# Loads of the down weights issued by ScalarE in place of SyncE, in a kernel of attention and a Hadamard FFN

## The reference

```python
x = x + LN(attention(LN(x)))     # 16 heads of 32, low-rank queries and values, rotary, softmax
x = x + LN(ffn(LN(x)))

def ffn(x):                      # 512 -> 2048 -> 512
    x = fwht(x * SU_ug) / 64
    up, gate = x @ W_up.T * (Wscale_ug[:2048] * 64), x @ W_gate.T * (Wscale_ug[2048:] * 64)
    x = fwht(silu(gate) * up * SU_dp) / 64
    return x @ W_down.T * (Wscale_dp * 64)
```

## Time and profile before

| | before |
|---|---|
| median of 3 runs | 2013.04 us (2004.34, 2013.72, 2013.04) |
| the profiled execution's own time | 2004.77 us |
| its span, first to last instruction | 2002.9 us |
| TensorE's granted clock over the span | 0.987 of 2.4 GHz |
| busy: PE, DVE, ACT, POOL | 94%, 64%, 55%, 47% |
| DMA engines, mean over the span | 140 GB/s |

### The profile page before, as it was taken

The page is one execution under the profiler, slowest core; times in us unless marked ns, Lnnn a source line. Parts: engine busy times, 40 slices in busy tenths (PEclk is TensorE's granted clock), DMA queues, the critical chain, the costliest instruction groups (busy, mean ns, idle before and its releaser), DMA issues.

```text
span 2002.9 us, 59647 instructions
## 1 busy us (share of the span) xinstructions
PE 1884.5 (94%) x24393; PEld 1364.1 (68%) x24393; DVE 1275.5 (64%) x2141; ACT 1094.4 (55%) x1731; POOL 937.6 (47%) x958
## 2 busy tenths in 40 slices
PE   2688999999999999999999999999999999999997
PEld 0355555777777777777767777777677776777786
DVE  6788666766677667666667667666666666654322
ACT  3557998555565554555556555555555555554221
POOL 3625545454465445544555446534555445443422
PEclk9799999999999999999999999999999999999999
DMA  8655623664457445664566445744556446533644
GB/s 222 193 153 129 168 51 72 163 145 121 121 147 177 116 119 139 155 162 121 137 171 150 127 112 140 176 121 136 138 149 161 121 130 157 138 107 107 192 140 128
DMA packets 353029, 280.95 MB, mean 140 GB/s; under 512 B 285216, under 2 KB 286496, under 8 KB 351776
## 3 DMA queue, kind: packets, MB, share of 16 engines
q1 hardware_dynamic: 343536, 265.83, 51.6%
q10 hardware_dynamic: 9264, 11.61, 2.0%
HBM read 189.30 MB, written 20.98 MB: 105 GB/s over the span
## 4 chain that ended last, share of the span: by engine, by line
PE 76%; DVE 6%; DMA 6%; SPq 5%; ACT 3%; issue 3%; ACTq 1%; POOL 1%; POOLq 0%; DVEq 0%
PE ps L842 29%; PE ps L866 14%; PE ps L784 5%; PE ps L772 5%; PE ps L796 5%; PE ps L812 4%; DMA qT<-tok 4%; PE ps L831 4%; SPq L592 3%; PE ps L686 2%; PE ps L817 2%; PE ps L738 2%; DVE mx L1326 1%; PE ps L674 1%; PE ps L750 1%
## 5 line engine op out<-in xcount | busy, mean ns | idle before, releaser
L1016 ACT ACTIVATE pr<-ps,exp_scale 128x1024 f16<-128x1024 f32 x256 | 285.4, 1115 | 360.3 <-PE ps L796 341.7
L1326 DVE TENSOR_REDUCE mx<-ps 128x2 f32<-128x1024 f32 x256 | 312.4, 1224 | 213.1 <-PE ps L784 211.9
L1437 POOL TENSOR_TENSOR pr<-p,pr 128x512 f16<-128x512 f32 x256 | 297.5, 1162 | 316.1 <-ACT p L1022 316.0
L842 PEld LDWEIGHTS ps<-x2T,gate_w 128*128 128x128 f16 x6144 | 362.3, 98 | 46.1 <-issue 10.7
L842 PEld LDWEIGHTS ps<-x2T,up_w 128*128 128x128 f16 x6144 | 359.6, 98 | 42.0 <-issue 13.4
L842 PE MATMUL ps<-x2T,gate_w 128*128 128x128 f16 x6144 | 387.3, 220 | 0.2 <-DVE room L1373 0.2
L842 PE MATMUL ps<-x2T,up_w 128*128 128x128 f16 x6144 | 386.9, 219 | 0.3 <-issue 0.2
L866 PE MATMUL ps<-room 128*128 128x512 f16 x1536 | 376.9, 382 | 6.6 <-POOL room L1465 5.4
L1465 POOL TENSOR_TENSOR room<-room 128x256 f16<-128x256 f32 x256 | 172.9, 675 | 309.9 <-ACT room L1052 308.9
L1047 ACT ACTIVATE room<-ps,half_gate 128x256 f32<-128x256 f32 x256 | 121.8, 476 | 265.9 <-PE ps L842 265.3
L1340 DVE TENSOR_TENSOR pr<-ps,pr 128x512 f16<-128x512 f32 x256 | 175.2, 685 | 115.1 <-ACT ps L1027 115.1
(11 more groups left out here) (191 smaller groups left out, 2446.2 us busy)
## 6 DMA issues: line engine op xcount, KB each, us to landing
room<-down_mid SPq DMA_DIRECT2D x256, 512.0 KB, 3.6
xr<-in_x SPq DMA_DIRECT2D x34, 256.0 KB, 4.0
y_mid<-xr SPq DMA_DIRECT2D x32, 256.0 KB, 2.3
room<-y_mid ACTq DMA_DIRECT2D x32, 256.0 KB, 2.8
xa<-in_x SPq DMA_DIRECT2D x30, 256.0 KB, 3.5
out<-room SPq DMA_DIRECT2D x24, 256.0 KB, 2.9
x2T<-in_W_gate SPq DMA_DIRECT2D x5, 1024.0 KB, 5.6
gate_w<-in_W_down SPq DMA_DIRECT2D x4, 1024.0 KB, 6.9
```

The lines of the kernel that those rows point to most:

```text
L842: mm = nc.tensor.matmul(ffn_ps[i % 2][:, col:col + P], weights[:, chunks[j // 4], kt, pw, j % 4 * P:(j % 4 + 1) * P], x2T[:, px, kt, t * P ...
L1016: nc.scalar.activation(pr[:, U % 2, 0].rearrange("p (j h) q -> p j (h q)", j=2), work[k], ACT.Exp, scale=exp_scale[:, 0:1]).then_inc(p_hi. ...
L1326: nc.vector.tensor_reduce(mx[:, 2 * tp:2 * tp + 2, h], work[k], AX.X, ALU.max).then_inc(sm_freed.sem, 1)
L1437: nc.gpsimd.tensor_tensor(lo, p32[:], hi, ALU.subtract).then_inc(p_low.sem, 1)
```

## The change

SP's lists lose every `wl` and SP's block loses the function. ScalarE's block gets it, without the wait for `down_done`, and `hid_` calls it at its end, so the load of item i is issued right behind ScalarE's step `hid.i`. The same function is also added to GpSimd's block, where nothing calls it. All other steps keep their places.

```diff
@@ ORDER, SP
-        wl.3@-1 stk.2.1 wl.4@-1 xl.0@1 wl.5@-1 xl.1@1 wl.6@-1 wl.7@-1 ln1.0@1 xl.2@1 wl.8@-1 wl.9@-1 ln1.1@1 xl.3@1
-        stq.2 wl.10@-1 rl.0 stk.3.0 wl.11@-1 ln1.2@1 stk.3.1 wl.12@-1 ln1.3@1 wl.13@-1 wl.14@-1 wl.15@-1 wl.16@-1
...
+        stk.2.1 xl.0@1 xl.1@1 ln1.0@1 xl.2@1 ln1.1@1 xl.3@1
+        stq.2 rl.0 stk.3.0 ln1.2@1 stk.3.1 ln1.3@1
...
@@ FRONT, SP
-        stk.0.1@1 raw.10 stq.0@1 raw.11 stk.1.0@1 stk.1.1@1 oe.0 rl.2 oe.1 oe.2 ln2.0 rl.3 wl.0 ln2.1 oe.3 wl.1 ln2.2
-        stq.1@1 wl.2 stk.2.0@1 ln2.3
+        stk.0.1@1 raw.10 stq.0@1 raw.11 stk.1.0@1 stk.1.1@1 oe.0 rl.2 oe.1 oe.2 ln2.0 rl.3 ln2.1 oe.3 ln2.2
+        stq.1@1 stk.2.0@1 ln2.3
@@ block.sync
-            def wl(b, i):
-                if first(b) and i < 2:
-                    sp.wait_ge(q_filled, 48)
-                    for k in range(2):
-                        sp.wait_ge(put[k], 16 * 8)
-                else:
-                    sp.wait_ge(*down_done.at(b, i - 2))
-                sp.dma_start(wr[:, i % 2], down_dram[i % (NJ // 2)].rearrange("p (j w n) -> p j w n", j=2, w=2)).then_inc(
-                    w_in[i % 2].sem, 16)
@@ block.scalar
+            def wl(b, i):
+                if first(b) and i < 2:
+                    sc.wait_ge(q_filled, 48)
+                    for k in range(2):
+                        sc.wait_ge(put[k], 16 * 8)
+                sc.dma_start(wr[:, i % 2], down_dram[i % (NJ // 2)].rearrange("p (j w n) -> p j w n", j=2, w=2)).then_inc(
+                    w_in[i % 2].sem, 16)
+
             def hid_(b, i):
                 sc.wait_ge(*f_freed.at(b, i))
                 sc.wait_ge(*down_done.at(b, i - 2))
                 nc.scalar.activation(hid[:, i % 2, 0, :], act[:, i % 2, :], ACT.Copy).then_inc(h_hi.sem, 1)
+                wl(b, i)
```

More of the change, by code:

```diff
@@ L119 @@
     SP="""
-        wl.3@-1 stk.2.1 wl.4@-1 xl.0@1 wl.5@-1 xl.1@1 wl.6@-1 wl.7@-1 ln1.0@1 xl.2@1 wl.8@-1 wl.9@-1 ln1.1@1 xl.3@1
-        stq.2 wl.10@-1 rl.0 stk.3.0 wl.11@-1 ln1.2@1 stk.3.1 wl.12@-1 ln1.3@1 wl.13@-1 wl.14@-1 wl.15@-1 wl.16@-1
-        wl.17@-1 stq.3 wl.18@-1 stk.0.0@1 wl.19@-1 stk.0.1@1 wl.20@-1 wl.21@-1 wl.22@-1 wl.23@-1 wl.24@-1 wl.25@-1
-        stq.0@1 wl.26@-1 rl.1 wl.27@-1 stk.1.0@1 wl.28@-1 stk.1.1@1 oe.0 fe.1@-1 wl.29@-1 oe.1 rl.2 wl.30@-1 ln2.0
-        wl.31@-1 rl.3 wl.0 ln2.1 wl.1 ln2.2 oe.2 oe.3 fe.2@-1 stq.1@1 wl.2 stk.2.0@1 fe.3@-1 ln2.3
+        stk.2.1 xl.0@1 xl.1@1 ln1.0@1 xl.2@1 ln1.1@1 xl.3@1
+        stq.2 rl.0 stk.3.0 ln1.2@1 stk.3.1 ln1.3@1
+        stq.3 stk.0.0@1 stk.0.1@1
+        stq.0@1 rl.1 stk.1.0@1 stk.1.1@1 oe.0 fe.1@-1 oe.1 rl.2 ln2.0
+        rl.3 ln2.1 ln2.2 oe.2 oe.3 fe.2@-1 stq.1@1 stk.2.0@1 fe.3@-1 ln2.3
     """,
@@ L613, in fe @@
                 sp.dma_start(out_v[b, t], yt[:, t % 2, :]).then_inc(out_done[t % 2].sem, 16)
-            parts = dict(lda=lda, ldv=ldv, wput=wput, wget=wget, ldx=ldx, raw=raw_, dst=dst, wl=wl, xl=xl, rl=rl, ln1=ln1, ln2=ln2, stk=stk, stq=stq, oe=oe, fe=fe)
+            parts = dict(lda=lda, ldv=ldv, wput=wput, wget=wget, ldx=ldx, raw=raw_, dst=dst, xl=xl, rl=rl, ln1=ln1, ln2=ln2, stk=stk, stq=stq, oe=oe, fe=fe)
             ahead = next(i for i, (b, s) in enumerate(FRONT["SP"]) if s[0] not in ("lda", "xl"))
```

## The result

The changed kernel takes 2179.14 us (median of 4 runs, 2162.27 to 2184.16) against 2009.62 for the kernel before on the same chip: **8.3% slower**, ratio 1.0825, interval [1.0779, 1.0871]. Forecast was 2060 us, with a range of 2024 to 2095. The sign was right; the loss of 170 us is three and a half times the 47 forecast.

The account below looks back on a forecast made before the run. TensorE was taken to bound the kernel. Terms of 33 - 21 + 11 + 20 + 5 = +48 us on the profiled execution gave 2060 us against the 2013 us median, range 2024 to 2095.

Parts of the forecast that it names:

- What bounds the kernel: Whole kernel: TensorE, busy for 94% of the span; only what makes it wait, or frees it, moves the time.
- ScalarE's issue, zero: ScalarE's 256 load issues of 0.344 us mostly hide behind `hid` computing; upper bound 88 us, taken as zero.
- Quiet price: From the start of `hid.i` to the first matmul with no transposition in flight: 3.4 us, ends 3.2 and 3.7.
- The sum for the tail: Batch 7, where FFN items run alone: late weights at short distances cost +20 us (14 to 27).
- Shortages in the loop, 5.5 us a pass: Six loop passes: late weights stall TensorE 5.5 us a pass, +33 us in all (15 to 60).
- What SP gives back: Loop passes: the queries' transposition is issued earlier without SP's loads, 3.5 us a pass, -21 us; bounds 0 and 26.
- Batch 6, +11: Unrolled back, 1690 to 1865 us: shorter distances, so late weights cost +11 us.
- Clock, +5: Longer TensorE waits in batches 6 and 7 bring half clock, three times 1.7: +5 us (0 to 10).
- rival C: Descriptor generator locked, so loads issued beside SP's transposition issues hold ScalarE: 36 us more, 2096 us; chance 0.05.
- E: Loads beside transpositions land at 6.7 us, SP's gain is nil: 2109 at the far end, 2085 to 2100 likelier; chance 0.15.
- Its sign of being wrong: Landings of 5 us and more with transpositions later than today would show the forecast wrong through crowding.
- B's relief: SP's relief at the queries' waits in the passes outweighs lateness: all 26 us back, 2001 us; chance 0.07.

Follow-up runs that it names:

- plain copies: Transpositions replaced by plain copies of as many bytes, softmax scale zero: 1985.97 us for the kernel before, 2042.32 us for the changed kernel.
- ScalarE at the old moments: Against the kernel before, ScalarE issues the loads, but at the moments at which SP did: 2001.3 us, ratio 0.9967.
- The guards: The changed kernel, with SP issuing three transpositions of each pass only when a load of ScalarE has landed: 2128.58 us, ratio 1.0615.
- the smaller pieces: The changed kernel with each partition's 4096 B of a load in pieces of 2048 B or 1024 B: 2135.89 us and 2130.92 us.
- the swap: The changed kernel with ScalarE's step reordered: wait for down.(i-2), issue the load, then wait for gate-up and make high halves: 2104.06 us.

## Why the prediction was wrong

By its own steps:

- **What bounds the kernel**: right. TensorE's waits, with the half clock behind them, took all of the loss; the busy time of VectorE, ScalarE and GpSimd stayed within 6 us.
- **ScalarE's issue, zero**: right in size (0.331 us at the median). But it hides more than I said: ScalarE's sequencer sends the load 0.29 us (median) before `hid` computes, up to 1.7 us where `hid` waits its turn, since the issue needs nothing of `hid`. I had "it can't start before `hid.i`". At items 5 and 6, for which stalls of 0.3 and 0.8 were summed, it is 0.93 us ahead, and they have none.
- **Quiet price, 3.4 us from `hid` to the matmul**: right. In batch 7, where TensorE waited for weights, it was 3.35 us at the median. The sum for the tail came out by two errors that cancel: its gaps are 20.1 us, of which 5.0 were there before, so 15 added and not 20; the half clock behind them makes it 24 on the stretch, where 5 were given to the clock in the whole kernel. That this total is right is luck in part.
- **Shortages in the loop, 5.5 us a pass**: the term for lateness was about right (4.3 with plain copies), though split otherwise: item 9 has 2.3, not 1.2. What failed is the upper bound for a load beside a transposition, "ends 3.7 and 6.7". Those landings come from a kernel in which the loads of the down weights leave early and stand in one queue with the transpositions; the changed kernel alters both. Item 11 was given a stall of 1.5 and has 6.2; items 10, 3 and 4, not in the sum, land in up to 14 us. The loop's gaps ahead of `down` are 83 us, not 33: **this is the step that failed**.
- **What SP gives back, -21**: wrong in sign. With ScalarE at the old moments SP did give something back, 1.8 us a pass in the loop instead of 3.5. In the changed kernel the wait at group 2 rises from 2.47 to between 3.7 and 8.8 us. The prediction said that the bytes "still move in the same stretch" but still priced the gain from SP's issues alone: the loads gone from ahead of the transposition came back beside it (item 3's is issued 0.65 us behind it and lands in 11.4 us in the pass from 1094.3, the transposition in 12.7).
- **Batch 6, +11**: 17, of which 13.7 are added gaps; the same mechanism in small.
- **Clock, +5**: 50 us of busy time is the real figure. It follows the waits, as in the earlier trace rows, but all along the loop, where I had taken the half clock as going away.
- **The lock rule (rival C)**: false here. ScalarE's load at 1163.62 was issued in 0.33 us inside SP's transposition issue of 6.42 us from 1161.59, as rows 8 had it. The Trainium skill (Perfetto Trace Analysis, DMA Instruction, HWDGE) has the generator locked for one sequencer at a time; the runs show no such hold. Of the 256 loads 49 were issued inside a transposition's issue, in 0.331 us at the median, as outside; three of them took 1.1 to 1.8 us, and those too were over before the transposition's issue was.
- **The rivals**: E (crowding, 0.15) named the mechanism, loads beside transpositions slow and transpositions delayed, but took 6.7 us as its worst landing and 2109 us as its far end. The slow landings turned out at 8 to 18 us. Its sign of being wrong, landings of 5 us and more with later transpositions, is what came. B's relief is what the run with early loads shows, at 0.3%.

In sum: +170 us is roughly +56 of lateness and +113 from the late loads and the transpositions slowing each other. The forecast had 69 of lateness and clock, less 21 given back. The second figure is the difference of two pairs of kernels, and that pair also changes the spacing on SP. The guards, the smaller pieces and the swap take 43 to 75 us away by the medians, each by another way; no single run takes away all of it. Not settled is why items 3 and 4 and, in some runs, 19 fall in, and how much of the waits for queries is bunching and how much follows from a late TensorE.

## What to carry to other kernels

A load's place in an instruction list sets not only when its data is there but also which transfers it meets: look at what the other queue has in flight at its new moment, and don't bound its landing by those of a kernel that issues it elsewhere. Moving the loads to the idle engine was free here, and a gain of 0.3%, with their moments kept; tied to the step just ahead of their use, they cost 8%. Where a load must be tied to a step, try its issue ahead of that step's other waits: here it gave back 75 of 170 us.

## What the runs showed of the hardware

- Two queues in one bunch slow each other far more than their bytes explain: the 512 KB load with no transposition in flight lands in 3.3 us at the median, beside transpositions in 3.1 to 6.7 in the two kernels that issue it early, in the bunch in 8 to 16, and the transposition in up to 18.5, where it was 8.1 at most. In the bunch the DMA engines moved 126 GB/s, just ahead of it 205. The Trainium skill (DMA: Bandwidth & Descriptors, Issuing engines are not separate DMA queues) says that DMAs of all engines interleave on the same 16 engines and that issuing from several only saves issue time. The early run agrees (0.3% gained); the changed kernel shows a cost that this leaves out.
- Smaller packets in one queue help the other: 4096, 2048 and 1024 B gave slowest transpositions of 18.5, 12.0 and 11.1 us, for 0.26 us more to issue (0.59 against 0.33) and a load of 3.4, 3.7 and 3.9 us (medians in batch 7).
- ScalarE's sequencer runs ahead of its compute: a DMA written behind an ACTIVATE was issued up to 1.7 us before that ACTIVATE started (0.29 at the median). SP, waiting for the same step's semaphore, issued it 0.44 us behind the start at the median.
